# One fp32r product over 96 stacked rows in place of a float32 product over 32 rows, at the end of a small circuit beside a large feed-forward stage

## What is computed

```python
ffn_out = x + gelu(x @ w1 + b1) @ w2 + b2             # 512 -> 2048 -> 512
angles  = f(x @ pd_w + pd_b)                           # 512 -> 4 wires
state   = product state of 16 amplitudes per row of x
state   = state @ U.T                                  # 16 x 16, complex
probs   = state.real**2 + state.imag**2
q_out   = (probs @ ZSIGN) @ pu_w + pu_b                # 16 -> 4 -> 512
# per batch: ffn_out or x + scale * q_out, chosen by vol; then two normalizations
```

## Time and profile before

| | us |
|---|---|
| median of 3 runs | 2577.67 |
| lowest and highest | 2573.52, 2578.06 |
| profiled execution, its own time | 2573.42 |
| its span, first to last instruction | 2571.6 |
| TensorE busy | 2424.2 |
| VectorE busy | 1342.5 |
| ScalarE busy | 990.1 |
| GpSimd busy | 982.8 |

### The profile page before, as it was taken

One profiled execution on the slowest core, in us unless ns is written; L12 is line 12 of the kernel. 1 busy time (PEld: TensorE's weight loads), 2 busy tenths in 40 slices (PEclk: granted clock), 3 DMA queues, 4 the chain that ended last, 5 costly groups with the idle time before them and its releaser, 6 DMA issues. The chain is left out here.

```text
span 2571.6 us, 44303 instructions
## 1 busy us (share of the span) xinstructions
PE 2424.2 (94%) x16100; PEld 1909.9 (74%) x16100; DVE 1342.5 (52%) x2700; ACT 990.1 (38%) x1977; POOL 982.8 (38%) x806
## 2 busy tenths in 40 slices
PE   5999999999998499999999999998589999999999
PEld 4687787777776367777777777776478888888887
DVE  5354454444444577777677667776433323333322
ACT  3231331331331376766666666666212111211211
POOL 0031431422422367767676667765022012102200
PEclk9999999999999699999999999999789999999999
DMA  5201101101101565555556555553411101110100
GB/s 166 75 17 58 41 16 57 41 16 57 41 1 41 188 185 177 178 190 162 180 166 200 162 173 177 174 171 126 153 56 50 49 0 49 49 49 0 49 33 17
DMA packets 133361, 243.69 MB, mean 95 GB/s; under 512 B 13212, under 2 KB 17452, under 8 KB 133184
## 3 DMA queue, kind: packets, MB, share of 16 engines
q1 hardware_dynamic: 133184, 241.39, 29.1%
HBM read 216.17 MB, written 25.20 MB: 94 GB/s over the span
## 5 line engine op out<-in xcount | busy, mean ns | idle before, releaser
L951 POOL TENSOR_TENSOR at_bias<-at_bias,at_mask 128x512 f32<-128x512 f32 x512 | 590.3, 1179 | 309.5 <-DMA at_bias<-in_fside_Bx16xSxS 270.8
L487 ACT ACTIVATE L_hid<-L_turn,L_b1c 128x512 f32<-128x512 f32 x256 | 176.2, 689 | 982.8 <-PE L_turn L285 977.7
L648 DVE CAST L_hh<-L_hid 128x512 fp32r<-128x512 f32 x256 | 123.6, 483 | 795.5 <-PE L_acc L746 756.8
L283 PE MATMUL L_turn<-L_xth,L_w1h 128*128 128x512 f32 x1024 | 406.5, 397 | 7.7 <-ACT L_hid L487 5.4
L744 PE MATMUL L_acc<-L_w2h,L_hh 128*128 128x512 f32 x1024 | 403.3, 394 | 7.6 <-DVE L_hl L650 7.6
L284 PE MATMUL L_turn<-L_xth,L_w1l 128*128 128x512 f32 x1024 | 400.6, 391 | 0.0
L746 PE MATMUL L_acc<-L_w2l,L_hh 128*128 128x512 f32 x1024 | 400.4, 391 | 0.0
L745 PE MATMUL L_acc<-L_w2h,L_hl 128*128 128x512 f32 x1024 | 400.3, 391 | 0.0
L285 PE MATMUL L_turn<-L_xtl,L_w1h 128*128 128x512 f32 x1024 | 400.0, 391 | 0.0
L982 ACT ACTIVATE at_bias<-at_bias,at_neg_top 128x512 f32<-128x512 f32 x512 | 362.9, 713 | 1.3 <-DVE at_neg_top L1105 1.3
L1105 DVE CUSTOM_DVE_ANT_0 at_bias<-at_score,at_bias 128x512 f32<-128x512 f32 x512 | 332.7, 684 | 50.1 <-PE at_score L1259 25.9
(11 more groups left out here) (206 smaller groups left out, 3036.1 us busy)
## 6 DMA issues: line engine op xcount, KB each, us to landing
at_bias<-in_fside_Bx16xSxS SPq DMA_DIRECT2D x256, 512.0 KB, 3.7
L_xin<-in_x SPq DMA_DIRECT2D x8, 1024.0 KB, 5.4
L_xres<-in_x SPq DMA_DIRECT2D x8, 1024.0 KB, 5.5
at_xin<-x_scratch SPq DMA_DIRECT2D x8, 1024.0 KB, 5.9
at_xres<-x_scratch SPq DMA_DIRECT2D x8, 1024.0 KB, 6.3
L_xin<-x_scratch SPq DMA_DIRECT2D x8, 1024.0 KB, 5.6
L_xres<-x_scratch SPq DMA_DIRECT2D x8, 1024.0 KB, 5.5
x_scratch<-L_xres SPq DMA_DIRECT2D x7, 1024.0 KB, 4.3
```

The costliest lines, as they stand in the source:

```text
L283: nc_mm = pe.matmul(out, ah, bh, start=i == 0, stop=False)
L951: nc.gpsimd.tensor_tensor(tile, tile, mask[:, m % TT, :], ALU.add).then_inc(masked, 1)
```

## The change

The last product takes 96 rows instead of 32 and is fp32r. The stationary side `stack` has the squares three times: rows 0 to 31 rounded, 32 to 63 their remainder, 64 to 95 rounded. The moving side `zpu` has its values rounded, rounded, and their remainder. One pass over 96 rows so adds rounded x rounded, remainder x rounded and rounded x remainder. To have the state three times in `misc[1]`, `keep.circuit` is three copies wide (16 x 96), and so is `zs` for the setup's product. ScalarE takes the squares twice (96 rows rounded into `stack`, and rows 32 to 63 in full into `prob`), and VectorE has a new step, `circuit_halves`, that makes the remainder. The rest of the diff shares buffers so that the copies fit.

```diff
-    LOADS = 9
+    LOADS = 11
...
-        self.rot2, self.part = sb("vrot2", [DIM, 2, DIM]), sb("vpart", [DIM, 2, DIM])
-        self.zs = sb("zs", [WIRES, 2 * DIM])
+        self.rot2 = self.part = sb("vrot2", [DIM, 2, DIM])
+        self.zs = sb("zs", [2 * DIM + WIRES, 3, 2 * DIM])[2 * DIM:, :, :]
...
-            (self.zs[:, :], c["zsign"]),
+            *((self.zs[:, i, :], c["zsign"]) for i in range(3)),
...
-        for column, phase, op in ((0, cos_b, ALU.subtract), (1, sin_b, ALU.add)):
-            nc.vector.scalar_tensor_tensor(keep.circuit[:, column * DIM:(column + 1) * DIM], re, phase, part[:, column, :],
-                                           ALU.mult, op).then_inc(self.circuit_set, 1)
-        nc.vector.tensor_copy(keep.zpu[:, :], self.banks[0][0:2 * DIM, :]).then_inc(self.circuit_set, 1)
+        for i in range(3):
+            for column, phase, op in ((0, cos_b, ALU.subtract), (1, sin_b, ALU.add)):
+                nc.vector.scalar_tensor_tensor(keep.circuit[:, i, column * DIM:(column + 1) * DIM], re, phase, part[:, column, :],
+                                               ALU.mult, op).then_inc(self.circuit_set, 1)
+        lo = slice(4 * DIM, 6 * DIM)
+        link(nc.vector.tensor_copy(keep.zpu[:, :], self.banks[0][0:6 * DIM, :]))
+        nc.vector.tensor_tensor(keep.zpu[lo, :], self.banks[0][lo, :], keep.zpu[lo, :].bitcast(F32), ALU.subtract)\
+            .then_inc(self.circuit_set, 1)
...
-            ampt = sb("ampt", [DIM, S])
-            prob = sb("prob", [2 * DIM, S])
+            amp_prob = sb("amp_prob", [4 * DIM, S])
+            ampt, prob = amp_prob[0:DIM, :], amp_prob[2 * DIM:4 * DIM, :]
+            stack = sb("stack", [6 * DIM, S], F32R)
...
-                        nc.scalar.activation(prob[:, :], misc[1][0:2 * DIM, :], ACT.Square).then_inc(prob_out, 1)
+                        nc.scalar.activation(stack[:, :], misc[1][0:6 * DIM, :], ACT.Square).then_inc(prob_hi, 1)
+                        nc.scalar.activation(prob, misc[1][2 * DIM:4 * DIM, :], ACT.Square).then_inc(prob_hi, 1)
...
+            def circuit_halves(b):
+
+                lo = slice(2 * DIM, 4 * DIM)
+                dve.wait_ge(prob_hi, 2 * b + 2)
+                nc.vector.tensor_tensor(stack[lo, :], prob, stack[lo, :].bitcast(F32), ALU.subtract).then_inc(prob_out, 1)
...
+                        if m == 11:
+                            circuit_halves(b)
...
-                    pe.matmul(misc[1][0:2 * DIM, :], keep.circuit[:, :], ampt[:, :], start=True, stop=True)\
+                    pe.matmul(misc[1][0:6 * DIM, :], keep.circuit[:, :, :].rearrange("p i j -> p (i j)"), ampt,
+                              start=True, stop=True)\
                         .then_inc(state_mm, 1)
...
-                    pe.matmul(misc[i % 2][:, :], prob[:, i * P:(i + 1) * P], keep.zpu[:, :], start=True, stop=True)\
+                    pe.matmul(misc[i % 2][:, :], stack[:, i * P:(i + 1) * P], keep.zpu[:, :], start=True, stop=True)\
                         .then_inc(up_mm, 1)
...
-                    pe.wait_ge(setup.circuit_set, 3)
+                    pe.wait_ge(setup.circuit_set, 7)
```

More of the change, by code:

```diff
@@ L109, in __init__ @@
         self.nc, self.keep, self.t, self.consts, self.scratch = nc, keep, t, consts, scratch
-        self.banks, self.wada, self.puw = banks, w_pass, ampt[0:WIRES, :]
+        self.banks, self.wada, self.puw = banks, w_pass, ampt
         self.ada = ada_row[0:B, :, :]
@@ L113, in __init__ @@
         self.freq = sb("freq", [P, 2])
-        self.ang, self.off, self.turns, self.sine, self.sig = (
-            sb(f"emb_{n}", [P, KT, B]) for n in ("ang", "off", "turns", "sine", "sig"))
+        self.ang, self.off, self.turns = (sb(f"emb_{n}", [P, KT, B]) for n in ("ang", "off", "turns"))
+        self.sine, self.sig = self.turns, self.off
         self.vol, self.qs = sb("vol", [P, B]), sb("qs", [P, 1])
@@ L267, in circuit_products @@
                          start=True, stop=True).then_inc(self.circuit_mm, 1)
-        nc.tensor.matmul(self.banks[0][0:2 * DIM, :], self.zs[:, :], self.puw, start=True, stop=True).then_inc(self.circuit_mm, 1)
+        nc.tensor.matmul(self.banks[0][0:6 * DIM, :], self.zs[:, :, :].rearrange("w i j -> w (i j)"), self.puw,
+                         start=True, stop=True).then_inc(self.circuit_mm, 1)
     def ada_product(self, pe, half):
@@ L339, in ffn_stage @@
             amp = sb("amp", [P, TT, DIM])
-            ampt = sb("ampt", [DIM, S])
-            prob = sb("prob", [2 * DIM, S])
+            amp_prob = sb("amp_prob", [4 * DIM, S])
+            ampt, prob = amp_prob[0:DIM, :], amp_prob[2 * DIM:4 * DIM, :]
+            stack = sb("stack", [6 * DIM, S], F32R)
             misc = [ps(f"misc{i}") for i in range(2)]
-            setup = Setup(nc, ctx, keep, t, table, scratch, misc, w_pass, ada_row, ampt, prob)
+            setup = Setup(nc, ctx, keep, t, table, scratch, misc, w_pass, ada_row,
+                          prob[0:WIRES, :], ampt)
             pd_set, p_mm, pt_out, p_turned, p_out, p_sig, halved, cs_out, amp_out, amp_turned, ampt_out, state_mm, \
-                prob_out, up_mm, up_added, row_set, ada_in = map(sem, (
+                prob_hi, prob_out, up_mm, up_added, row_set, ada_in = map(sem, (
                     "pd_set", "p_mm", "pt_out", "p_turned", "p_out", "p_sig", "halved", "cs_out", "amp_out", "amp_turned",
-                    "ampt_out", "state_mm", "prob_out", "up_mm", "up_added", "row_set", "ada_in"))
+                    "ampt_out", "state_mm", "prob_hi", "prob_out", "up_mm", "up_added", "row_set", "ada_in"))
         across = lambda n: t[n].partition_broadcast(P)
@@ L505, in body @@
                         act.wait_ge(amp_turned, b + 1)
-                        nc.scalar.activation(ampt[:, :], misc[0][0:DIM, :], ACT.Copy).then_inc(ampt_out, 1)
+                        nc.scalar.activation(ampt, misc[0][0:DIM, :], ACT.Copy).then_inc(ampt_out, 1)
                     if l0 and m == 11:
                         act.wait_ge(state_mm, b + 1)
-                        nc.scalar.activation(prob[:, :], misc[1][0:2 * DIM, :], ACT.Square).then_inc(prob_out, 1)
+                        nc.scalar.activation(stack[:, :], misc[1][0:6 * DIM, :], ACT.Square).then_inc(prob_hi, 1)
+                        nc.scalar.activation(prob, misc[1][2 * DIM:4 * DIM, :], ACT.Square).then_inc(prob_hi, 1)
                     if not l0 and not last and m == 6:
@@ L1396, in __init__ @@
         self.ident = sb("ident", [P, P])
-        self.circuit = sb("circuit", [DIM, 2 * DIM])
-        self.zpu = sb("zpu", [2 * DIM, D])
+        self.circuit = sb("circuit", [DIM, 3, 2 * DIM])
+        self.zpu = ctx.enter_context(nc.sbuf_tensor("zpu", [6 * DIM, D], F32R))
         self.take_q = sb("take_q", [P, B])
```

## The result

The changed kernel takes 2543.39 us in the median of six runs (2537.63 to 2551.67), the kernel before 2577.86 (2573.52 to 2580.76). The ratio is 0.987 with a 95% interval of 0.985 to 0.989: 27 to 39 us less. The profiled execution took 2545.35, its span is 2543.6 against 2571.6 before.

What follows compares the result with a forecast made beforehand. TensorE's stream was taken to bound the first stage's full batches. Gains of 24.5, 1.0 and 6.7 (32.2 us) less costs of 0.4, 0.1 and 0.6 gave 31.1 us, so a 2545 us median; range 2538 to 2555.

Steps and rivals of the forecast that it cites:

- The gap and its two parts: Around each last product on TensorE: 1.02 us beyond one fp32r product, 0.63 for float32's two passes, 0.39 for changing form.
- the form change: Both sides of the last product: late stationary load and longer step behind, 0.39 us, going with row number, not float32.
- the first rival: Last product: 96 rows are a mode of their own, the drain stays, only 19 us gained; chance 0.09.
- Where the batch ends: Transposes behind seven last products: 0.96 us gained each, 6.7 in all; slack falls from 1.3 to about 0.6, nothing lost.
- The new step on VectorE: `circuit_halves` at m = 11, behind `hl` and ahead of the next `hh`: ends by 307.6 to 308.6, costs nothing.
- The rival that ends slower: VectorE stands in `circuit_halves`, delaying `hh` and `down`; needs it 13 us later than worked out; near 2590 us; chance 0.02.
- the second rival: A new wait, L569 or `prob_out` late: at 1 us a batch 7 us lost, 24 remain; chance 0.07.
- The fourth, that nothing moves: Whole kernel: the time is taken back at another place, so no gain; chance 0.02.
- The wider state product: Circuit's float32 product of 16 rows, stationary side from 32 to 96 columns: costs 0.05 us a batch, 0.4 in all.
- The wait at `m = 8` of batch 0: Setup: longer making of `zpu` adds 1.4 to 1.5 us against 0.9 free; TensorE waits about 0.6 us, once.
- The sum: First stage: 32.2 us gained, less 0.4, 0.1 and 0.6, net 31.1 us, about 3.8 a batch.
- a sign of being wrong: Profile after: the later stages change length by some us at the same work, though taken as unchanged.

Runs made afterwards that it cites:

- the version with both products in fp32r: Changed kernel with the state product also one fp32r pass over 96 rows; median 2540.85 us, ratio 0.986 to the kernel before.
- the run with the additions alone: Changed kernel with the last product back to float32 over 32 rows, everything added around it kept; median 2578.72 us, ratio 1.000 to the kernel before.

## Why the prediction was right

**The gap and its two parts.** 1.02 us were forecast for each last product with an `up` behind it; the timeline shows 1.70 to 0.70, 1.00. The split stands on runs of its own: with the form change left and the float32 pass gone 1.07 remain (0.63 less), with the pass left and the form change gone 1.33 (0.37 less). They were forecast as 0.63 and 0.39. That 96 rows count as the whole array was the choice that the sum rested on. It was argued from three kinds of rows and is now shown: no idle time put down to issue at 96 rows, 11.3 us of it at 64 and at 32. So the first rival falls. The Trainium skill (TensorEngine Tiling (Array Packing), Available Configurations) lists row tiles of 32 and of 64 rows and the whole array, and does not name 96; the runs agree with the list as the prediction read it. The runs show the gap and where it stands; that the array is drained in it they don't show.

**What the rows alone leave out.** The prediction says that the gap goes with the number of rows. The trace of before has it in one more place, around setup's product at `m = 8`, which has all 128 rows but only 8 stationary columns:

```profile
82.86 0.39 PE L746 MATMUL L_acc<-L_w2l,L_hh 128*128 128x512 f32 x1
83.18 0.10 PEld L274 LDWEIGHTS L_misc<-L_w_pass,su_emb_sig 128*8 128x8 f32 x2 [0.35 <-issue]
...
86.71 0.50 PE L283 MATMUL L_turn<-L_xth,L_w1h 128*128 128x512 f32 x1
87.05 0.40 PE L284 MATMUL L_turn<-L_xth,L_w1l 128*128 128x512 f32 x1
```

Again the load comes 0.35 after the last one ended, and the step behind is 0.34. It can't be the rows there. The transposes of the amplitudes, 128 rows and 16 columns, show no such time (L761: 1.7 us ahead of 32 loads, none put down to issue). No run varied the columns of a product with all its rows, so which numbers of columns bring the gap is open. The forecast didn't need it, since the last product has 128 columns before and after.

**Where the batch ends.** L746 to L744 was to fall from 2.21 to 1.25. It is 321.25 - 319.99 = 1.26 in the timeline of TensorE after:

```profile
319.99 0.39 PE L762 MATMUL L_acc<-L_w2l,L_hh 128*128 128x512 f32 x1
320.22 0.40 PE L790 MATMUL L_misc<-zpu,L_stack 96*128 96x512 f32 x1
320.45 1.04 PE L740 MATMUL L_turn<-ident,L_xin 128*128 128x128 f32 x8
321.25 0.48 PE L760 MATMUL L_acc<-L_w2h,L_hh 128*128 128x512 f32 x1
```

No transpose waits for VectorE; its two remainders of the input end at 323.49 and the second group of transposes starts at 324.08, a cover of 0.6 as worked out.

**The new step on VectorE.** The rows of VectorE and ScalarE at `m = 11` after:

```profile
297.66 1.66 DVE L664 TENSOR_TENSOR L_hl<-L_hid,L_hh 128x512 fp32r<-128x512 f32 x1
299.35 1.67 DVE L622 TENSOR_TENSOR L_stack<-L_amp_prob,L_stack 32x512 fp32r<-32x512 f32 x1
303.35 0.43 DVE L662 CAST L_hh<-L_hid 128x512 fp32r<-128x512 f32 x1 [2.33 <-PE L_acc L762]
```

It follows `hl` at once and ends at 301.02, 2.06 us ahead of the product that needs it (2.2 forecast) and 2.3 ahead of the next `hh`. It takes 1.67 in seven batches of eight, the dearer of the two prices that were kept open, since GpSimd is at work; in batch 0, where GpSimd is idle at that place, it took 0.68. The cost is nothing, as said, and the run with two more subtractions shows how much room is left. The rival that ends slower needed this step to be late, and the second rival needed this or the transposes' wait for L569; neither came. The fourth, that nothing moves, falls with the stage's end, which came 31.2 us earlier.

**The small costs.** The wider state product costs 0.06 a batch (0.05 forecast): L762 to L288 around it is 297.51 - 296.16 = 1.35 us where it was 1.29. The wait at `m = 8` of batch 0 is the term that was most mis-sized:

```profile
82.50 0.69 DVE L238 TENSOR_TENSOR zpu<-L_misc,zpu 32x512 fp32r<-32x512 f32 x1
82.71 0.39 PE L762 MATMUL L_acc<-L_w2l,L_hh 128*128 128x512 f32 x1
83.25 3.60 PE L279 MATMUL L_misc<-L_w_pass,su_emb_off 128*8 128x512 f32 x8
```

TensorE's `ada_product` (L279) starts 0.54 us after L762 where it took 0.32 before, so 0.2 are lost, not 0.6. The six phase instructions follow each other in 0.93 in place of the 1.1 that was reckoned, and VectorE came to them 0.4 earlier (80.55, before 80.93). It is 0.4 of 31 us.

**The sum.** 31.1 were forecast for the first stage, whose end moved by 31.2. Of these, 0.4 come from a start that was earlier in this execution. SyncE's issue of batch 1's input, before and after:

```profile
65.94 0.51 SPq L388 DMA_DIRECT2D L_xin<-in_x  x1
...
65.58 0.51 SPq L395 DMA_DIRECT2D L_xin<-in_x  x1
```

From there to the stores the stage is 780.17 - 749.35 = 30.8 us shorter. The terms as measured add up to that: 25 x 1.00 + 7 x 0.95 - 8 x 0.06 - 0.1 - 0.2 = 30.9 (the 0.1 is the forecast's own bound for setup's other product). So the terms were right to some tenths, and that 31.1 and 31.2 are so close is luck in the last 0.4.

The forecast for the whole took the later stages as unchanged. Their work is, but their length is not: in ten profiles the attention stage took 964 to 978 us. In this pair it took 1.9 us more and the third stage 1.3 more. The prediction had named that as a sign of being wrong, "if the later stages change length by some us at the same work", and the sign came: the profiled execution took 2545.35, not the 2542.3 that were worked out for it. The change's worth in the first stage was right; the step from it to the whole time was not exact. So the agreement of the median (2543.39 for 2545) is partly luck, and the stage marks are the better evidence.

## What to carry to other kernels

A product of 64 rows or fewer between products of 128 rows paid twice here, for itself and for the change of form around it. 96 rows cost less than 32 even in the same number of passes, so in a stream that TensorE bounds it can pay to fill the rows with something useful, such as the remainder terms of a split product. Look at the idle time put down to issue ahead of the product's load first: it shows whether there is a gap to win, and it also stood ahead of a product with few columns.

Price a small product by the starts of its neighbours, not by its record, and judge a change in one stage by that stage's own marks when other stages scatter by as much as the gain.

## What was not expected of the hardware

**A short wait can cost as much again.** In the run with six more subtractions TensorE stood for about 2 us once a batch. In three of the seven batches this was followed by a stretch at a lower clock. Windows over one of them (length, busy by engine, granted clock before the DMA share), around the wait that starts near 402.7:

```profile
402.00:405.00 3.00, 0.84 (x5) 0.37 (x3) 2.84 (x5) 0.00 (x0) 0.00 (x0) 1.00 0.00 0
405.20:409.20 4.00, 4.00 (x12) 3.10 (x11) 1.46 (x3) 0.00 (x0) 0.00 (x0) 0.57 0.00 0
409.20:412.00 2.80, 2.80 (x14) 2.33 (x13) 0.00 (x0) 0.69 (x1) 0.00 (x0) 1.00 0.00 0
```

The mean of 0.57 over 4 us says that most of the stretch was at half of full speed, 1.2 GHz: products start 0.43 apart there instead of 0.23. Such a batch takes 98.1 in place of 96.2 to 96.5, 1.8 us more on top of 2.0 of waiting. The last batch has such a stretch too:

```profile
794.70:797.90 3.20, 3.20 (x9) 2.49 (x8) 0.51 (x1) 0.00 (x0) 0.00 (x0) 0.52 0.02 5
```

TensorE was busy up to the wait in these batches as in the others. In order of the batches the waits lasted 2.16, 1.85, **2.16**, 2.08, **2.17**, 1.89 and **1.72** us, with the lower clock behind those in bold. The shortest was followed by it and the first was not, so the length of the wait alone does not decide, and what does is not shown.

**The same stage at the same work is not equally long.** The attention stage, windows from the first stage's end to the third's start, in the version with both products in fp32r:

```profile
807.00:1785.00 978.00, 913.30 (x9472) 701.31 (x9472) 685.13 (x1580) 625.04 (x1477) 629.59 (x544) 0.95 0.56 173
```

and in the run with the additions alone:

```profile
848.00:1812.00 964.00, 899.71 (x9472) 692.29 (x9472) 685.60 (x1580) 624.92 (x1477) 629.86 (x544) 0.97 0.56 175
```

VectorE, ScalarE and GpSimd are busy for the same time to within 0.5 us; TensorE's granted clock is 0.95 in one and 0.97 in the other. The clock of the changed kernel's six timed runs goes with their time as well, 0.976 at 2537.63 and 0.971 at 2551.67. That the place at which the attention stage starts has a part in this was not tried.
